# Image statistics summed by accumulating DMAs in a vision tower kernel, with graph preparation, strips and waits rearranged

## The reference, cut to what matters

```python
# x: 64 images, 2 channels, 104 x 104
concat = concat(x, left_up(x), right_up(x), left_down(x), right_down(x))  # 10 channels, shifts by 4, zeros moved in
mean, var = per image over all 10 channels
normed = (concat - mean) * rsqrt(var + 1e-7) * gamma + beta
h = conv 8x8, stride 8, 10 -> 128 channels: 13 x 13 tokens; class token in front: 170 tokens of 128 per image
h = h + graph_layer(layernorm(h))     # 1 -> 4 -> 1 graph convolutions over 128 nodes, 1024 edges, then Wp
z = layernorm(h)
y = causal attention(LN(z), 2 heads, l2-normalised q and k)
h = h + sum over 8 experts of softmax gate * (gelu(y W1 + b1) W2 + b2)
```

## Time and profile before

| | |
|---|---|
| median of 3 runs | 1624.26 us (1622.1 to 1627.21) |
| profiled execution | 1623.35 us, span 1621.6 us |
| granted TensorE clock, mean | 0.976 |
| busy: PE, DVE, ACT, POOL | 93%, 75%, 68%, 13% |
| start, to the first gamma product of a strip | 0 to 28.57 us |
| strips, to the last convolution | 28.57 to 174.24 us |
| attention 0 | 174.24 to 205.76 us |
| group 0's experts | 205.76 to 277.10 us |

### The profile page before, as it was taken

One profiled execution on the slowest core, in us unless ns is written; L12 is line 12 of the kernel. 1 busy time (PEld: TensorE's weight loads), 2 busy tenths in 40 slices (PEclk: granted clock), 3 DMA queues, 4 the chain that ended last, 5 costly groups with the idle time before them and its releaser, 6 DMA issues.

```text
span 1621.6 us, 31694 instructions
## 1 busy us (share of the span) xinstructions
PE 1502.3 (93%) x10879; PEld 1027.2 (63%) x10879; DVE 1222.6 (75%) x2549; ACT 1104.0 (68%) x1925; POOL 207.5 (13%) x211
## 2 busy tenths in 40 slices
PE   6788899998999989998999999999989999999998
PEld 4455666666666666666666666666666666666665
DVE  7878886877868777777768687767778687867665
ACT  4222576776767778676767777776767777777766
POOL 3125033010101001010101010010101010010101
PEclk9899899999999999999999999999999999999979
DMA  4222043333314243333324242332323142333323
GB/s 169 76 84 74 1 144 57 96 43 87 47 34 102 35 104 43 96 44 94 44 47 87 32 106 41 96 52 87 43 72 67 26 112 35 99 49 96 53 87 53
DMA packets 35937, 114.01 MB, mean 70 GB/s; under 512 B 5248, under 2 KB 5248, under 8 KB 33664
## 3 DMA queue, kind: packets, MB, share of 16 engines
q0 software_dynamic: 18432, 44.57, 20.4%
q1 hardware_dynamic: 17120, 67.71, 11.5%
q10 hardware_dynamic: 288, 0.77, 0.1%
HBM read 62.56 MB, written 50.48 MB: 70 GB/s over the span
## 4 chain that ended last, share of the span: by engine, by line
PE 53%; DVE 20%; issue 7%; ACT 3%; DVEq 1%; DMA 1%; POOLq 0%; ACTq 0%
PE pair L981 21%; PE pair L962 17%; PE pair L749 5%; DVE area L1374 3%; DVE area L1296 3%; PE pair L874 2%; DVE root_t L1216 2%; DVE area L1303 2%; DVE area L1386 1%; PE pair L777 1%; PE pair L908 1%; PE pair L901 1%; PE pair L859 1%; DVE area L1372 1%; PE pair L830 1%
## 5 line engine op out<-in xcount | busy, mean ns | idle before, releaser
L613 ACT ACTIVATE area<-pair,pack_b_sb 128x680 f32<-128x680 f32 x512 | 422.7, 828 | 261.3 <-PE pair L962 232.2
L981 PE MATMUL pair<-area,ws 128*128 128x340 f16 x3072 | 534.4, 309 | 45.5 <-DVE area L1374 31.7
L1374 DVE TENSOR_TENSOR area<-area 128x680 f16<-128x680 f32 x512 | 442.6, 868 | 146.1 <-ACT area L618 140.5
L962 PE MATMUL pair<-area,ws 128*128 128x340 f16 x3072 | 532.7, 310 | 0.0
L981 PEld LDWEIGHTS pair<-area,ws 128*128 128x128 f16 x3072 | 285.8, 98 | 204.9 <-DVE area L1386 43.2
L962 PEld LDWEIGHTS pair<-area,ws 128*128 128x128 f16 x3072 | 299.8, 99 | 146.8
L618 ACT ACTIVATE area<-pair,pack_b_sb 128x680 f16<-128x680 f32 x384 | 316.2, 823 | 0.0
L446 POOL DMA_DIRECT2D tower_out<-area x128 | 109.7, 857 | 1213.6 <-DVE area L1386 1136.8
L1386 DVE SCALAR_TENSOR_TENSOR area<-pair,pack_b_sb,area 128x340 f32<-128x340 f32 x256 | 134.0, 565 | 29.9 <-PE pair L981 17.3
L577 ACT ACTIVATE area<-pair,nbias,root 85x85 f32<-85x85 f32 (+1 forms) x256 | 112.4, 464 | 22.9 <-DVE nbias L1284 22.9
L736 PE MATMUL pair<-area,pack_a_sb 128*128 128x392 f32 (+1 forms) x260 | 95.2, 508 | 28.6 <-DVE area L1203 19.0
(11 more groups left out here) (211 smaller groups left out, 1666.2 us busy)
## 6 DMA issues: line engine op xcount, KB each, us to landing
tower_out<-area POOLq DMA_DIRECT2D x128, 340.0 KB, 4.6
area<-gate_scratch SPq DMA_DIRECT2D x16, 1360.0 KB, 10.4
area<-gate_scratch SPq DMA_DIRECT2D x16, 1020.0 KB, 7.2
area<-cells SPq DMA_DIRECT2D x14, 392.0 KB, 3.3
tower_out<-ht SPq DMA_DIRECT2D x16, 340.0 KB, 2.3
area<-gate_scratch SPq DMA_DIRECT2D x16, 340.0 KB, 4.6
area<-cells SPq DMA_DIRECT2D x13, 364.0 KB, 3.8
stage_sb<-w SPq DMA_DIRECT2D x16, 256.0 KB, 5.3
```

What stands on the lines that cost most here:

```text
L613: nc.scalar.activation(two(hid[slot % NHID]), halves(hid_ps[slot % 2]), ACT.Gelu_apprx_tanh, bias=col(COL_B1 + slot)).then_inc(hid_ready, 1)
L962: last = mm(hid_ps[slot % 2][:, j, 0:TH], lhs[:, w], rhs[:, j * TH:(j + 1) * TH], start=(i == 0), stop=(i == 2))
L981: last = mm(eo_ps[:, j, 0:TH], lhs[:, w], rhs[:, j * TH:(j + 1) * TH], start=(m % CH == 0 and i == 0), stop=(m % CH == CH - 1 and i == 2))
L1374: v.tensor_tensor(hl[slot % NPART], hid[slot % NHID], hh[slot % NPART], ALU.subtract).then_inc(hlo_ready, 1)
```

## The change

1. `sum_x` and `rim_x` start as loads of row 0 by SP. GpSimd then issues for each further row an accumulating DMA from HBM into `sum_x` and one from `sq1` into `sum_sq`, each behind the landing of the one before; for the last row also the two rims. GpSimd's and VectorE's additions are gone. ScalarE squares one row further ahead. Two of the weight splits now stand between the rows (`W_SPLIT`), loads of weights begin at strip 6.
2. `sums_rest` is cut into five parts behind points 60 to 64; `image_factors(1, ...)` stands ahead of attention 0, with its matmul in another bank.
3. The block of graph preparation at point 17 is cut into five pieces behind points 17, 18, 20, 25 and 28.
4. From strip 5 on, odd strips use the banks `hid_ps[0]` (free once preparation is done), and the first convolution waits for the copy of two strips back.
5. In the loop VectorE drops the wait for `chunk_used` where ScalarE made the high part, and the repeated waits for `gate_in` within one transfer.

```diff
-W_ROW = 8
+W_ROW = 6
+W_SPLIT = (9, 11)
+ALONE = 4
-DVE_PREP = {4: 1, 6: 2, 9: 3, 17: 5}
+DVE_PREP = {4: 1, 6: 2, 9: 3, 17: 5, 18: 6, 20: 7, 25: 8, 28: 9}
+DVE_SUMS = {60: 0, 61: 1, 62: 2, 63: 3, 64: 4}
...
-        def cells_ps(j):
-            return eo_ps[:, j, 0:(CELLS[j][1] - CELLS[j][0]) * BZ]
+        def cells_ps(p, j):
+            pair = hid_ps[0] if p > ALONE and p % 2 else eo_ps
+            return pair[:, j, 0:(CELLS[j][1] - CELLS[j][0]) * BZ]
...
-                    sp.wait_ge(xsum_done, a - R1 + 2)
...
+            for dst in (sum_x, rim_x):
+                sp.dma_start(dst, cells1[0]).then_inc(xrow_in, 16)
...
-            for a in range(NG1):
-                pool.wait_ge(row1_in[a % R1], 16 * (a // R1 + 1))
...
-                    pool.tensor_tensor(sum_x, sum_x, row1[a % R1], ALU.add).then_inc(xsum_done, 1)
...
+            for a in range(1, NG1):
+                if a == 1:
+                    pool.wait_ge(xrow_in, 32)
+                else:
+                    pool.wait_ge(xsum_done, 16 * (a - 1))
+                pool.dma_start(sum_x, cells1[a], accum_op=ALU.add).then_inc(xsum_done, 16)
+                if a == NP:
+                    pool.dma_start(rim_x, cells1[a], accum_op=ALU.add).then_inc(rim_step, 16)
+                pool.wait_ge(xsq_done, a + 2)
+                if a > 1:
+                    pool.wait_ge(sqsum_done, 16 * (a - 1))
+                pool.dma_start(sum_sq, sq1[a % 2], accum_op=ALU.add).then_inc(sqsum_done, 16)
+                if a == NP:
+                    pool.dma_start(rim_sq, sq1[a % 2], accum_op=ALU.add).then_inc(rim_step, 16)
+                if a in W_SPLIT:
...
+                    split(W_SPLIT.index(a))
+            for e in range(len(W_SPLIT), 4):
                 split(e)
...
-                    act.wait_ge(sqsum_done, a - 2)
+                    act.wait_ge(sqsum_done, 16 * (a - 2))
...
+            squares(1)
...
-                if shift == 0:
-                    squares(p + 1)
+                if shift == 0 and p + 2 < NG1:
+                    squares(p + 2)
...
-                    if shift == 0 and p:
+                    if shift == 0 and 0 < p <= ALONE:
                         pe.wait_ge(tok_done, 2 * (p - 1) + j + 1)
+                    if shift == 0 and p == ALONE + 1:
+                        pe.wait_ge(act_prep, PREP_ACT)
+                    if shift == 0 and p > ALONE + 1:
+                        pe.wait_ge(tok_done, 2 * (p - 2) + j + 1)
...
-                if n % SHIFTS == SHIFTS - 1:
-                    square_sum(n // SHIFTS + 1)
                 chain(n)
                 if n in DVE_PREP:
                     prepare(DVE_PREP[n])
+                if n in DVE_SUMS:
+                    sums_rest(DVE_SUMS[n])
             for n in LATE:
                 chain(n)
-            sums_rest()
+            image_factors(1, BZ, BA, hid_ps[1][:, 1, 0:2 * BZ])
             attention(0, False, True)
...
-                if slot >= NPART:
-                    dve.wait_ge(chunk_used, n - NPART + 1)
                 if hi_on_act(slot):
                     dve.wait_ge(hhi_act, his(g, slot + 1))
                 else:
+                    if slot >= NPART:
+                        dve.wait_ge(chunk_used, n - NPART + 1)
...
-                part = [n for n, (e0, e1) in enumerate(GATE_PARTS) if e0 <= e < e1][0]
-                dve.wait_ge(gate_in[part], 16 * (g + 1))
+                for n, (e0, e1) in enumerate(GATE_PARTS):
+                    if e == e0:
+                        dve.wait_ge(gate_in[n], 16 * (g + 1))
```

More of the change, by code:

```diff
@@ L855, in values @@
                     pe.wait_ge(hhi_act, his(g, 0))
+                if b == 3 and not later:
+                    pe.wait_ge(img_step[1], 3)
                 for k in range(2):
@@ L1026, in _ @@
                 chain(n)
+            image_stats(1, BZ, hid_ps[1][:, 1, 0:2 * BZ])
+            pe.wait_ge(tok_done, 2 * NP - 2)
             attention(0, False, True)
-            pe.wait_ge(dev2_ready, 2)
-            image_stats(1, BZ, fr_ps[:, 1, 0:2 * BZ])
             with pe.Fori(1, G - 1) as g:
@@ L1141, in sums_first, with sums_rest @@
                 v.scalar_tensor_tensor(whole, whole, 5.0, stats[0][:, 2 * BA:4 * BA], ALU.mult, ALU.add).then_inc(part_step[0], 1)
-            def sums_rest():
+            def sums_rest(k):
                 stat = stats[1]
-                dve.wait_ge(xsum_done, NG1 + 2)
-                dve.wait_ge(sqsum_done, NG1)
-                sums, rims, side_sums, side_rims = (stat[:, k * 2 * BZ:(k + 1) * 2 * BZ] for k in (1, 2, 3, 0))
-                for n, (whole, rim) in enumerate(((sum_x, rim_x), (sum_sq, rim_sq))):
-                    for a, full, side in ((whole, sums, side_sums), (rim, rims, side_rims)):
-                        v.tensor_reduce(full[:, n * BZ:(n + 1) * BZ], a.rearrange("p (c b) -> p b c", b=BZ),
-                                        AX.X, ALU.add).then_inc(stat_step, 1)
-                        v.tensor_tensor(side[:, n * BZ:(n + 1) * BZ], a[:, 0:BZ], a[:, N1 - BZ:N1], ALU.add).then_inc(stat_step, 1)
+                sums, rims, side_sums, side_rims = (stat[:, n * 2 * BZ:(n + 1) * 2 * BZ] for n in (1, 2, 3, 0))
+                if k < 4:
+                    if k == 0:
+                        dve.wait_ge(xsum_done, 16 * NP)
+                    if k == 1:
+                        dve.wait_ge(sqsum_done, 16 * NP)
+                    if k == 2:
+                        dve.wait_ge(rim_step, 32)
+                    n, a = k % 2, (sum_x, sum_sq, rim_x, rim_sq)[k]
+                    full, side = (sums, side_sums) if k < 2 else (rims, side_rims)
+                    v.tensor_reduce(full[:, n * BZ:(n + 1) * BZ], a.rearrange("p (c b) -> p b c", b=BZ),
+                                    AX.X, ALU.add).then_inc(stat_step, 1)
+                    v.tensor_tensor(side[:, n * BZ:(n + 1) * BZ], a[:, 0:BZ], a[:, N1 - BZ:N1], ALU.add).then_inc(stat_step, 1)
+                    return
                 dve.wait_ge(stat_step, 8)
```

49 lines of the change are left out of this document (17 added, 32 removed).

## The result

| | before | changed |
|---|---|---|
| median on the same chip | 1625.68 us (1622.1 to 1627.21) | 1567.53 us (1564.85 to 1570.0) |
| ratio | | 0.9645, 95% interval 0.962 to 0.967 |
| span of the profiled execution | 1621.6 us | 1568.2 us |
| granted TensorE clock, mean | 0.976 | 0.985 |

What follows compares the result with a forecast made beforehand. It took TensorE, waiting on VectorE and ScalarE in the strips, as the bound. Start 1.2, strips 16.5, closing sums 1.0, factors 2.8 and loop 1 sum to 22.5 us: forecast 1602 us, range 1593 to 1610.

Steps and rivals of the forecast that it cites:

- Loop body: VectorE's loop: dropped waits are mostly hidden behind products or gelu waits; gain 1 us, bounds 0 and 24.
- Rival B: VectorE's loop: the dropped waits are on the path, half of 24 us more gained, 1590 us; chance 0.12.
- Strips: Convolution of strips: stage falls from 145.7 to 129 us, gain 16.5, bounds 8.5 and 26.5.
- busy term: Convolution of strips: TensorE's busy time falls from 117.0 to 109 us, at 2.4 GHz throughout.
- idle term: Convolution of strips: 20.2 us lost to hand-overs on top of the fuller engine's busy time, kept unchanged.
- Sums: Strips: accumulating DMAs replace additions, landing in 5.3 us (bounds 3.3 and 8.2), costing the path and VectorE nothing.
- rival C: Strips: slow accumulation into SBUF sets the pace, 1654 us at 14 us per sum; chance 0.06.
- Start: Before the strips: VectorE's five first products no longer run beside GpSimd's additions; gain 1.2 us, bounds 0 and 3.3.
- Banks and pieces: Strips: alternate banks remove 3.7 us of ScalarE waits; cutting up graph preparation recovers 4.3 of a 5.32 us hole.
- Closing sums and factors: After the last convolution: attention 0 begins 1.0 us sooner, group 0's experts lose a 2.8 us wait.
- A: Strips: the relief turns into VectorE idle time, total 1610 to 1619, say 1615 us; chance 0.18.
- D: Whole kernel: no change, the removed work was hidden throughout, 1624 us; chance 0.04.

Runs made afterwards that it cites:

- e3: Changed kernel with the 26 waits put back into VectorE's loop body; 1566.6 us, ratio 0.9632.
- r1: Changed kernel run once more, unaltered; 1565.5 us, ratio 0.964.
- p4: Changed kernel with GpSimd's weight splits moved behind rows 10 and 12, the other two after the last convolution; 1566.3 us, ratio 0.9642.
- s1: Changed kernel without GpSimd's first four weight splits; ScalarE writes high parts and plain copies as low parts, no subtraction; 1558.2 us, ratio 0.9607.
- p3: Changed kernel with the sums back on the engines, x on GpSimd and squares on VectorE; 1584.0 us, ratio 0.9743.
- e1: Kernel before with only the loop's wait edit, 26 instructions fewer in VectorE's loop body; 1589.1 us, ratio 0.9772.
- e4: Changed kernel with 56 more satisfied wait instructions far ahead of the untouched loop; 1599.5 us, ratio 0.9829.
- q2: Changed kernel with 48 more satisfied wait instructions ahead of the loop; 1599.9 us.
- q1: Changed kernel with 40 more satisfied wait instructions ahead of the loop; 1620.0 us.
- e2: Kernel before, loop body untouched, with 50 more satisfied wait instructions far ahead of the loop; 1591.6 us, ratio 0.9792.
- q3: Changed kernel with 34 more satisfied wait instructions ahead of the loop; 1563.2 us.
- v1: p4 with the splits of experts 2 and 3 behind VectorE's first subtraction of group 0; 1563.3 us, ratio 0.9628.

## Why the prediction was wrong

**Loop body: the step that failed.** The prediction counted 26 waits, priced each by what it issues (0.07 us) and hid them behind a product. As far as it goes that is true: e3 gives 0.07 us a turn for all. But "TensorE is busy 86.8" of a 90.7 us turn was taken as the turn's nature, and "nothing in the change touches what TensorE does in a group". In that turn TensorE waited at the branch for the stalled VectorE (2.4 us of its 3.9 idle), and in a turn without low clock it is busy only 85.5. The stall itself, 2.8 us a turn on VectorE, stood in two rows of the page that no step read: the CAST group with 33.7 us of "issue", and 78 code transfers where a program that is read once needs under 20. What was changed was not the waits' time but the program's length, and the place of the loop in it. The miss here, 34.7 us instead of 1, is more than the whole error of the spans (53.4 instead of 22.5); all other terms together came 2.8 us short. Rival B named a place on the path and had a price of 12 us; its mechanism, the waits' issue, is refuted too.

The Trainium skill, "Runtime: NRT & Kernel Launch", Instruction fetch mechanics, says that a taken branch whose target is not in the window of loaded code forces a fetch before execution goes on, and that an engine other than TensorE holds 512 instructions. The traces agree with the first: 2.7 to 3.6 us a branch. It gives blocks of 256 instructions; VectorE's transfers here are of 8 KB, 128 instructions, and a loop of 310 could stall or not. That fits the 512 if a loop's three blocks and one read ahead make four, which no run here shows. By it the prediction would have had a rival: all 33.7 us of "issue" gone, 1601.8 - 33.7 = 1568 us.

**Strips: right in mechanism, 8 us too good, and the cause was named and not priced.** The forecast took TensorE's busy time at full clock, 109, plus 20.2: 129. Its own bound "if the clock stays as it is" was 137, and that is what came in the profiled execution, 137.1 at 0.93, with 119.6 busy and 17.5 idle (r1: 132.5 at 0.96, with 115.0 busy). The busy term was the one mis-sized, by 10.6 us; even at a clock of 1.00 it is 111 (p4, s1), not 109. The idle term was 2.7 us too high. The prediction's sentence that the splits "keep costing as before" was right, but it priced them by VectorE's excess alone. Their cost is the hole they make when VectorE is no longer far ahead, and the half-clock matmuls behind it: with them elsewhere, stages of 125.0 to 128.9 us in six kernels at a clock of 0.99 to 1.00 where it was read.

**Sums.** Landing 4.8 and 6.5 us in the median (5.3 forecast, bound 8.2); neither VectorE nor ScalarE waits for one. The longest took 10.4 us, over the 9.9 named as a sign of rival C, without a wait. The products' mean in s1, with all 28 accumulating DMAs and no splits, is 909 ns against a fastest of 903 and a slowest of 921: they cost VectorE nothing, as forecast. Worth some 16 us by p3.

**Start** 3.2 instead of 1.2: all five products take 1.57 us now, so its bound of 3.3 came, not the 1.2. **Banks and pieces** 0 to 5 us each against 3.7 and 4.3: not refuted. **Closing sums and factors** 8.3 instead of 3.8: the maxima start 4.0 instead of 5.5 us behind the last convolution (1.5, forecast 1.0), and all 3.7 us of the factors left the place ahead of group 0's first split (forecast 2.8). The other 3.1 us lie inside attention 0. There TensorE's clock was 1.00 instead of 0.89 and its busy time 24.1 instead of 27.4 us, which no term counted.

**Rivals.** A described the strips in this execution better than the forecast did. C and D are refuted. Without the loop the forecast would have stood: e1, which is before with the loop's stall gone, is at 1589.1 and the changed kernel at 1567.5, 21.6 us less (by the ratios 20.6), and the sum of all other terms was 21.5. That agreement is in part luck: the strips came 8 us short in the profile, the start and attention 0 came 6.5 us over, and the strips stage moves by 5 us from one execution to the next.

## What to carry to other kernels

Count a loop body's instructions per engine and look for idle time put down to "issue" right behind its branch and for code transfers that grow with the turns; a few instructions fewer, or harmless ones more ahead of the loop, can be worth more than the rest of an edit, here some 35 of 58 us. When helper work runs on GpSimd, ask which VectorE instructions it stands beside: chains of short ones pay the most and hand their wait on. After an edit to straight code, compare the time of a loop that was not touched.

## What the runs showed of the hardware

- VectorE's code comes in 8 KB transfers. A loop whose body ends up to 375 instructions behind the start of its first block of 128 ran free; from 381 on each branch back cost 2.7 to 3.6 us, in five transfers a turn.
- TensorE's granted clock was at the lower level for stretches of 3.4 or 6.8 us, behind waits at the branch such as the 2.34 us above, in 6 (before, e4), 7 (q2) and 10 (q1) of the twelve stalling turns, and in no turn of the changed kernel, e1, e2, e3 and q3. In before they did not lengthen the turn.
- Within those limits neither the body's length (284 or 310) nor 26 satisfied waits in it changed a turn by over 0.25 us.
- Beside a GpSimd split a VectorE step of 56 columns took up to 1.22 us instead of 0.22 and one of 8 columns 1.01 instead of 0.16; TENSOR_SCALAR steps with one SBUF input also, 0.58 instead of 0.17 us in v1 and 0.93 instead of 0.19 in p4. In p4's image factors and v1's root steps each slowed step ends within 0.07 us of the end of the GpSimd instruction beside it, as if it waited for the whole of it; one whose other input lies in PSUM (L1185, first line) was not slowed. From p4, and the GpSimd instruction beside both:

```profile
150.88 0.22 DVE L1185 TENSOR_TENSOR statz<-pair,statz 128x56 f32<-128x56 f32 x1
151.13 0.93 DVE L1187 TENSOR_SCALAR statz<-statz 128x56 f32<-128x56 f32 x1
150.86 1.15 POOL L424 TENSOR_TENSOR ws<-stage_sb,ws 128x512 f16<-128x512 f32 x1
```

  and from v1:

```profile
178.66 0.58 DVE L1228 TENSOR_SCALAR root<-root_in 85x8 int32<-85x8 int32 x1
```

  The Trainium skill, "SBUF — State Buffer", Who interferes with whom, excludes an instruction with one SBUF input unless it is in a two-port mode; whether these are in such a mode no run here shows.
- Twenty-eight accumulating DMAs into SBUF of 392 KB landed in 3.9 to 10.4 us; in s1, without splits, no VectorE product beside them took over 921 ns.
